# Latent attention on one core: two heads' keys in one tile, and score products in the halves of the array

## The chip, the cores and the metric

The kernel runs on one core of one Trainium2 chip. The metric is the device time of one execution in microseconds (us); less is better. Five engines run their own instruction lists and meet at semaphores: TensorE (PE, with its weight loads PEld), VectorE (DVE), ScalarE (ACT), GpSimd (POOL) and SyncE (SP).

## The reference

Two transformer layers on x of 1024 tokens by 256 features. The change touches the third of four blocks, the latent attention:

```python
    x = x + _layernorm(_L0_attn_ref(_layernorm(x, axis=-1), L0_attn_w_qkv, L0_attn_w_out), axis=-1)
    x = x + _layernorm(_L0_ffn_ref(_layernorm(x, axis=-1), L0_ffn_W_up, L0_ffn_W_gate, L0_ffn_W_down), axis=-1)
    x = x + _layernorm(_L1_attn_ref(_layernorm(x, axis=-1), L1_attn_Wdq, L1_attn_Wuq, L1_attn_Wdkv, L1_attn_Wuk, L1_attn_Wuv, L1_attn_Wo), axis=-1)
    x = x + _layernorm(_L1_ffn_ref(_layernorm(x, axis=-1), L1_ffn_lut, L1_ffn_gate_idx, L1_ffn_up_idx, L1_ffn_down_idx), axis=-1)
...
            c_kv = x @ Wdkv.T
            q = (x @ Wdq.T @ Wuq.T).reshape(B, T, nh, hs).transpose(0, 2, 1, 3)
            q_lat = jnp.einsum('bhtd,hdl->bhtl', q, k_eff)
            scores = jnp.einsum('bhtl,bsl->bhts', q_lat, c_kv) / jnp.sqrt(jnp.float32(hs))
            scores = jnp.where(causal[None, None, :, :], scores, jnp.finfo(scores.dtype).min)
            attn = jax.nn.softmax(scores, axis=-1)
            ctx = jnp.einsum('bhts,bsl->bhtl', attn, c_kv)
            y = jnp.einsum('bhtl,hld->bhtd', ctx, v_eff)
```

There are 16 heads of 16 features each, T is 1024, and the mask is causal.

## The kernel before

The whole program is written out by hand. Four lists of steps (`HEADS`, `FFN0`, `LATENT`, `FFN1`) are made before anything is issued; each engine walks the same lists in the same order and issues its part of each step. `order_of_latent` merges lists by hand-given costs, so the order of the work is fixed when the program is built. Matmul results go to PSUM banks that are handed out from a ring of six in the order of the list (`take_ring`); a bank comes free when the instruction that is marked for it has read it.

The latent attention works on eight pairs p of heads (2p and 2p+1). A head needs only 16 features, but each operand is kept as a high and a low part, so 48 or so of 64 partitions are in use for a head, and a pair fills 128 partitions: the even head the lower 64, the odd head the upper 64. For a pair:

- **project** (L1311): two matmuls of 512 columns for each half of the tokens, for q (`which` 0) and for k (`which` 1).
- q: ScalarE writes the rounded part to `R1` (L1603), VectorE writes the finished operand from the PSUM bank and `R1` with one instruction (L1920) to `QT(p)`. This frees the bank.
- k: ScalarE writes `R1` (L1603) and a second copy, `R2` (L1608, its tile is called `tern` in the trace). The bank is free after that. The keys are then `R2 - R1`, made by two instructions of 64 partitions each, one for each head: by VectorE for pair 0 (L1929), by GpSimd for pairs 1 to 7 (L2161). They go to two separate tiles, `KT[p % 4][:, 0]` and `[:, 1]`. Each tile has 128 partitions, of which the other head's 64 were set to zero (`keys_zero`, L2029). So a score product can take all 128 rows of q: the other head's q meets zeros.
- **row_max** (L1323): scores of 128 queries against up to 512 keys; VectorE adds the mask and takes the row maximum (L1947, with an instruction that reads the accumulator behind it). Even and odd head alternate in the list.
- **shift** (L1333, transposes): the maxima are turned, and VectorE subtracts them inside q (L1957).
- **weights** (L1344; L1369 for the last four heads): transposed scores, 128 keys against up to 1024 queries, in one or two products. ScalarE takes the exponential (L1617; L1627), GpSimd masks the diagonal block (L2168; L2175).
- **combine** (L1358; L1383): weights times values. Four heads stand side by side in the array's columns, 32 each (`tile_position=(0, 32 * j)`).

Three groups of four heads run this way, each beside the row maxima and projections of the pairs that come next; the last group runs beside the splitting of the weights of the next block (`split_gu`, `split_dn`). R1 has three buffers. `KT` has four pairs of tiles, so pairs 4 to 7 wait until the pair four before them is used up.

## Time and profile before

| | |
|---|---|
| median of 3 runs | 925.1 us (924.72 to 926.01) |
| profiled execution, span from first to last instruction | 923.3 us |
| TensorE busy | 832.7 us (90%), 4330 matmuls |
| VectorE busy | 766.5 us (83%) |
| ScalarE busy | 605.9 us (66%) |
| GpSimd busy | 430.6 us (47%) |

The profile is of one execution. Its own device time is not listed beside it; the three timed runs are 1.4 to 2.7 us above its span, which is what lies around the first and the last instruction. An engine is busy while it works on an instruction, also when that instruction is one of several in flight. The chain of work that ended last is followed back from the end: each piece was released by the piece before it, so its shares tell which engine set the time there. The latent attention runs from about 660 to 863 us of the span.

### The profile page before, as it was taken

To read this page: it belongs to the slowest core of one execution; us is meant where nothing else is said; L and a number is where in the kernel's file an instruction comes from. 1 tells how busy PE (TensorE), PEld (TensorE's weight loads), DVE (VectorE), ACT (ScalarE), POOL (GpSimd) and SP (SyncE) were. 2 spreads that over 40 slices of the span, in tenths; PEclk is the share of its full clock that TensorE was granted. 3 is DMA by queue.
4 is the path that set the end of the run, shared out by engine and by line. 5 is a ranking of instruction groups with operands and counts; after the bars stand their busy time and mean duration, and the time that the engine had idled before them with its cause. 6 is when DMAs were issued, how large, how long until landed. Compare 5 with 4: busy or idle time off the path is not lost.

```text
span 923.3 us, 13156 instructions
## 1 busy us (share of the span) xinstructions
PE 832.7 (90%) x4330; PEld 534.6 (58%) x4330; DVE 766.5 (83%) x1597; ACT 605.9 (66%) x1042; POOL 430.6 (47%) x455
## 2 busy tenths in 40 slices
PE   3889999999999999989899998679788999998997
PEld 2555665665665565655565565457555555554686
DVE  3788999889989999999899998585598687876637
ACT  5677767777777676766667767374545767657531
POOL 3134354354445277787667771171323434433301
PEclk9999999999999999999999999799989999999999
DMA  3388858966977667857857668130000000000001
GB/s 122 78 184 156 143 117 190 163 126 136 206 134 153 130 131 144 166 110 144 157 103 132 136 130 159 24 106 0 1 1 1 1 0 2 0 2 1 1 1 45
DMA packets 276867, 86.29 MB, mean 93 GB/s; under 512 B 267584, under 2 KB 272448, under 8 KB 276416
## 3 DMA queue, kind: packets, MB, share of 16 engines
q1 hardware_dynamic: 275520, 80.05, 44.8%
q0 software_dynamic: 992, 5.34, 1.9%
q8 instruction: 34, 0.56, 0.3%
q14 instruction: 33, 0.27, 0.1%
q10 hardware_dynamic: 288, 0.07, 0.0%
HBM read 17.29 MB, written 1.05 MB: 20 GB/s over the span
## 4 chain that ended last, share of the span: by engine, by line
PE 40%; DVE 37%; issue 9%; ACT 8%; DMA 3%; POOL 1%; SPq 1%; POOLq 0%; DVEq 0%; ACTq 0%
DVE EP L1762 9%; DVE nmax L1747 8%; PE ps L1097 7%; PE ps L1099 7%; PE ps L1098 7%; PE ps L1120 4%; DVE ptm L1861 3%; PE ps L1358 3%; PE ps L1344 3%; PE ps L1135 3%; PE ps L1323 3%; DVE ps L1947 2%; DMA ET<-EP 2%; DVE OL L1821 2%; DVE st L1661 1%
## 5 line engine op out<-in xcount | busy, mean ns | idle before, releaser
L1523 ACT ACTIVATE EP<-ps,rinv 128x1024 f16<-128x1024 f32 x128 | 142.2, 1112 | 44.5 <-DVE rinv L1757 42.9
L1762 DVE SCALAR_TENSOR_TENSOR EP<-ps,rinv,EP 128x1024 f16<-128x1024 f32 x128 | 163.3, 1276 | 2.4 <-ACT EP L1523 2.0
L1513 ACT ACTIVATE ps<-ps,nmax 128x1024 f32<-128x1024 f32 x128 | 139.2, 1088 | 35.7 <-DVE nmax L1747 35.2
L1747 DVE TENSOR_REDUCE nmax<-ps 128x1 f32<-128x1024 f32 x128 | 155.0, 1211 | 0.7 <-PE ps L1099 0.7
L1097 PE MATMUL ps<-KH,QH 128*128 128x512 f32 x256 | 115.4, 451 | 8.3 <-DVE KL L1729 4.2
L2106 POOL TENSOR_TENSOR wgu<-wgu,ptm 128x688 f32<-128x688 f32 x60 | 99.7, 1661 | 45.8 <-DVE ptm L1861 43.7
L1097 PE MATMUL ps<-ET,VH 128*128 128x512 f16 x256 | 98.7, 385 | 17.8 <-DMA ET<-EP 14.2
L1099 PE MATMUL ps<-KH,QL 128*128 128x512 f32 x256 | 100.8, 394 | 0.0
L2106 POOL TENSOR_TENSOR wdn<-wdn,ptm 128x512 f32<-128x512 f32 x45 | 57.7, 1282 | 92.2 <-DVE ptm L1861 91.0
L1098 PE MATMUL ps<-KL,QH 128*128 128x512 f32 x256 | 100.5, 392 | 0.0
L1098 PE MATMUL ps<-ET,VH 128*128 128x512 f16 x256 | 98.3, 384 | 0.0
L1099 PE MATMUL ps<-ET,VL 128*128 128x512 f16 x256 | 98.3, 384 | 0.0
L1617 ACT ACTIVATE ET<-ps 128x512 f32<-128x512 f32 (+3 forms) x144 | 62.6, 497 | 37.6 <-PE ps L1344 37.0
L1947 DVE CUSTOM_DVE_ANT_0 ps<-ps,tern 128x512 f32<-128x512 f32 (+3 forms) x128 | 71.9, 603 | 15.5 <-PE ps L1323 15.4
L2013 POOL TENSOR_TENSOR rs<-ve,mhalf 128x4 f32<-128x4 f32 (+2 forms) x22 | 19.8, 898 | 122.4 <-DVE ve L1666 98.2
L1097 PEld LDWEIGHTS ps<-KH,QH 128*128 128x128 f32 x256 | 48.2, 188 | 27.8 <-DVE EP L1762 8.1
L2168 POOL TENSOR_SCALAR_AFFINE_SELECT ET<-ET 128x128 f32<-128x128 f32 x96 | 28.1, 292 | 65.1 <-ACT ET L1617 58.3
L1097 PEld LDWEIGHTS ps<-ET,VH 128*128 128x128 f16 x256 | 25.8, 101 | 54.2 <-DMA ET<-EP 16.2
L1099 PEld LDWEIGHTS ps<-KH,QL 128*128 128x128 f32 x256 | 48.0, 188 | 11.1
L1097 PE MATMUL ps<-xh,wqh 128*128 128x512 f16 x128 | 49.8, 389 | 4.0 <-DVE KL L1729 3.4
L1098 PEld LDWEIGHTS ps<-KL,QH 128*128 128x128 f32 x256 | 48.3, 189 | 7.3
L1098 PE MATMUL ps<-xl,wqh 128*128 128x512 f16 x128 | 49.1, 384 | 0.0
(250 smaller groups left out, 2126.7 us busy)
## 6 DMA issues: line engine op xcount, KB each, us to landing
wqr<-in_wqk SPq DMA_DIRECT2D x16, 256.0 KB, 3.6
wgu<-in_tern POOLq DMA_DIRECT2D x3, 1024.0 KB, 6.1
wvr<-in_wv SPq DMA_DIRECT2D x8, 256.0 KB, 3.9
wor<-in_wo SPq DMA_DIRECT2D x16, 128.0 KB, 3.1
ET<-EP SPq DMA_TRANSPOSE x128, 4.3
X<-in_x SPq DMA_DIRECT2D x2, 512.0 KB, 5.7
prw<-in_down_idx POOLq DMA_DIRECT2D x2, 256.0 KB, 7.0
tern<-in_l_wuq_rep SPq DMA_DIRECT2D x1, 512.0 KB, 4.5
```

Source lines behind the costliest of these rows:

```text
L1097: e.matmul(dst, lh, rh, start=first, stop=False)
L1098: e.matmul(dst, lh, rl, start=False, stop=False)
L1099: return e.matmul(dst, ll, rh, start=False, stop=last)
L1120: mm = e.matmul(ps[:, 2 * r + o, :], l, m, start=i == 0, stop=i == len(pairs) - 1)
L1513: e.activation(bank, bank, ACT.Exp, bias=nmax[:, c:c + 1], scale=1.0, accum_out=rsum[:, c:c + 1]).then_inc(exped.sem, 1)
L1523: e.mul(EP[:, n % NE_RING, 0, :], SB(u, j), rinv[:, c:c + 1]).then_inc(e_hi.sem, 1)
L1617: e.activation(ET[:, r, c:c + n1], ps[:, BANK[(*step, c)][0], n - n1:n], ACT.Exp).then_inc(weight_exped.sem, 1)
L1747: e.tensor_reduce(nmax[:, c:c + 1], SB(u, j), AX.X, ALU.max, negate=True).then_inc(maxed.sem, 1)
L1762: e.scalar_tensor_tensor(out=EP[:, n % NE_RING, 1, :], in0=SB(u, j), scalar=rinv[:, c:c + 1], in1=EP[:, n % NE_RING, 0, :], op0=ALU.mult, ...
L1947: e.tensor_tensor_reduce(src, src, mask[:, m0:m0 + n], 1.0, -3.0e38 if part == 0 else half, ALU.add, ALU.max, NM[:, p % 2, i8, col:col + 1 ...
L2106: e.tensor_tensor(dst, dst, ptm[:, v % 2, 0:n], ALU.add).then_inc(lut_added.sem, 1)
L2168: e.affine_select(out=tile, in_=tile, compare_op=ALU.is_ge, fill=0.0, base=0, pattern=[[1, P]], channel_multiplier=-1).then_inc(masked.sem, 1)
```

## The change

The keys of a pair now lie in one tile of 128 partitions, even head below, odd head above, without zeros. So there are eight tiles, one for each pair, in the same memory. A score product takes only the 64 rows of its head and is placed in the lower or the upper half of the array's rows (`tile_position=(64 * hh, 0)`). The keys are split by one VectorE instruction straight from PSUM, as q is; `R2`, its ScalarE copies, the GpSimd subtractions and the zeroing are gone. The bank of a k projection is now freed by VectorE, not by ScalarE. The two weight tiles of the last block that lie in the same memory wait for other heads than before.

```diff
-             ("fold_k", 1), ("keys_zero", 3), ("split",), ("fold_v",), ("turn_in", b1, 1),
+             ("fold_k", 1), ("split",), ("fold_v",), ("turn_in", b1, 1),
...
-        KT = [QH, QL, KH, KL]
+        KT = [t[:, i, :] for t in (KL, QH, QL, KH) for i in range(2)]
...
-        GL = [KT[m // 2][:, m % 2, :] for m in range(4)]
+        GL = KT[0:4]
...
+        def rows_of(h):
+            return slice(64 * (h % 2), 64 * (h % 2) + 64)
...
-                if which == 0:
-                    r1_free[r] = q_split.mark(p, half)
-                    take_ring(step, q_split[p, half])
-                else:
-                    r2 = take(step, "r2", 2)
-                    R2_OF[step] = (r2, r2_free[r2])
-                    take_ring(step, k_lo_in.mark(p, half))
-                    for hh in range(2):
-                        token = (k_split_v if p == 0 else k_split_g).mark(2 * p + hh, half)
-                    r1_free[r] = r2_free[r2] = token
+                r1_free[r] = (q_split, k_split)[which].mark(p, half)
+                take_ring(step, r1_free[r])
...
-                    w.wait_ge(*k_split(h, 0))
-                    w.wait_ge(*k_split(h, (c + n - 1) // 512))
-                    e.matmul(ps[:, i, 0:n], QT(p)[:, i8 * P:i8 * P + P], KT[p % 4][:, hh, c:c + n],
-                             start=True, stop=True).then_inc(max_scored.sem, 1)
+                    w.wait_ge(*k_split[p, 0])
+                    w.wait_ge(*k_split[p, (c + n - 1) // 512])
+                    e.matmul(ps[:, i, 0:n], QT(p)[rows_of(h), i8 * P:i8 * P + P], KT[p][rows_of(h), c:c + n],
+                             start=True, stop=True, tile_position=(64 * hh, 0)).then_inc(max_scored.sem, 1)
...
-                        e.matmul(ps[:, i, 0:n], KT[p % 4][:, h % 2, k * P:k * P + P], Q2[p % 4][:, q0:q0 + n],
-                                 start=True, stop=True).then_inc(weighed.sem, 1)
+                        e.matmul(ps[:, i, 0:n], KT[p][rows_of(h), k * P:k * P + P], Q2[p % 4][rows_of(h), q0:q0 + n],
+                                 start=True, stop=True, tile_position=(64 * (h % 2), 0)).then_inc(weighed.sem, 1)
...
-                    if which == 1:
-                        r2, freed = R2_OF[step]
-                        w.each([freed])
-                        e.activation(R2[:, r2, :], bank, ACT.Identity, scale=pat[:, 5:6]).then_inc(k_lo_in.sem, 1)
...
-                    elif p == 0:
-                        r2 = R2_OF[step][0]
-                        w.wait_ge(*k_lo_in[p, half])
-                        w.wait_ge(*zeroed["keys", 0, 1])
-                        for hh in range(2):
-                            rows = slice(64 * hh, 64 * hh + 64)
-                            e.tensor_tensor(KT[0][rows, hh, cs], R2[rows, r2, :], f32(R1[rows, r, :]),
-                                            ALU.subtract).then_inc(k_split_v.sem, 1)
+                    else:
+                        w.wait_ge(*l1_hi[step])
+                        e.scalar_tensor_tensor(out=KT[p][:, cs], in0=ps[:, BANK[step][0], :], scalar=pat[:, 5:6],
+                                               in1=f32(R1[:, r, :]), op0=ALU.mult,
+                                               op1=ALU.subtract).then_inc(k_split.sem, 1)
...
-                    for h in range(8, 12):
+                    for h in range(4 * (m // 2), 4 * (m // 2) + 4):
                         w.wait_ge(*weighed[h, 7, "last"])
```

The GpSimd branch of L2148 to L2162 and `keys_zero` are removed as well, and the products of the last group (L1369) are changed as those of L1344.

**VectorE, the first projections of pairs 0 and 1** (the keys' tile is `QH` before and `KL` after, q's is `Q`; L1920 became L1898, L1947 became L1922). Before:

```order
L1682 TENSOR_TENSOR X<-X,XN 128x256 x2
L1929 TENSOR_TENSOR QH<-tern,R 64x512 x2
L1920 SCALAR_TENSOR_TENSOR Q<-ps,pat,R 128x512
L1661 BN_STATS st<-X 128x6 x2
L1664 BN_AGGR mv<-st 128x2 x2
L1666 TENSOR_SCALAR ve<-mv 128x2
L1672 TENSOR_SCALAR nm<-mv 128x2
L1920 SCALAR_TENSOR_TENSOR Q<-ps,pat,R 128x512
L1947 ISA ps,NM<-ps,tern 128x128
```

After:

```order
L1660 TENSOR_TENSOR X<-X,XN 128x256 x2
L1903 SCALAR_TENSOR_TENSOR KL<-ps,pat,R 128x512
L1898 SCALAR_TENSOR_TENSOR Q<-ps,pat,R 128x512
L1639 BN_STATS st<-X 128x6 x2
L1642 BN_AGGR mv<-st 128x2 x2
L1644 TENSOR_SCALAR ve<-mv 128x2
L1650 TENSOR_SCALAR nm<-mv 128x2
L1903 SCALAR_TENSOR_TENSOR KL<-ps,pat,R 128x512
L1898 SCALAR_TENSOR_TENSOR Q<-ps,pat,R 128x512
L1922 ISA ps,NM<-ps,tern 128x128
```

Two instructions of 64 partitions gave way to one of 128 for pair 0, and pair 1 has one ahead of its q that GpSimd did before.

**VectorE, the projections of pair 4 among the row maxima of pair 3** (738 to 744 us of the trace; the tile written for pair 4's keys is `QL` after). Before:

```order
L1920 SCALAR_TENSOR_TENSOR XH<-ps,pat,R 128x512
L1947 ISA ps,NM<-ps,tern,M 128x256
L1947 ISA NM 128x1
L1947 ISA ps,NM<-ps,tern,M 128x256
L1947 ISA NM 128x1
L1947 ISA ps,M<-ps,tern 128x512
L1947 ISA M 128x1
```

After:

```order
L1898 SCALAR_TENSOR_TENSOR XH<-ps,pat,R 128x512
L1922 ISA ps,NM<-ps,tern,M 128x256
L1922 ISA NM 128x1
L1922 ISA ps,NM<-ps,tern,M 128x256
L1922 ISA NM 128x1
L1903 SCALAR_TENSOR_TENSOR QL<-ps,pat,R 128x512
L1922 ISA ps,M<-ps,tern 128x512
L1922 ISA M 128x1
```

The split of the keys stands in line with the row maxima. The same happens twice for every pair from 2 to 7.

**GpSimd, from the first group on** (`ET` holds the exponentials that it masks). Before:

```order
L2161 TENSOR_TENSOR QL<-tern,R 64x512 x4
L2168 AFFINE_SELECT ET<-ET 128x128
L2161 TENSOR_TENSOR KH<-tern,R 64x512 x2
L2168 AFFINE_SELECT ET<-ET 128x128 x2
L2161 TENSOR_TENSOR KH<-tern,R 64x512 x2
L2168 AFFINE_SELECT ET<-ET 128x128 x6
```

After:

```order
L2113 AFFINE_SELECT ET<-ET 128x128 x96
L2120 AFFINE_SELECT ET<-ET 128x128
L2126 MEMSET KL 128x80
L2120 AFFINE_SELECT ET<-ET 128x128 x5
L2126 MEMSET KL 128x80
```

Only the masks are left, and the small memsets of `split_gu` stand behind the same masks as before. TensorE's list keeps its order and its number of matmuls; only operands and places in the array change.

## Rows read from the trace of the kernel before

**Rows 1.** Windows: length, then busy us of PE, PEld, DVE, ACT, POOL; clock; DMA.

```profile
660.00:711.00 51.00, 38.12 (x147) 24.91 (x146) 45.35 (x148) 27.66 (x50) 16.05 (x20) 0.93 0.00 1
711.00:830.00 119.00, 113.59 (x659) 65.83 (x657) 93.51 (x309) 79.33 (x171) 52.46 (x112) 0.99 0.01 1
830.00:863.00 33.00, 29.18 (x170) 13.64 (x170) 18.90 (x56) 25.01 (x60) 14.24 (x40) 1.00 0.00 1
```

**Rows 2.** Chain of work that ended last, by line: 711 to 830, 830 to 863 us.

```profile
by line: PE ps L1358 23.1%; PE ps L1344 21.5%; PE ps L1323 17.0%; DVE ps L1947 9.4%; issue 6.6%; ACT ET L1617 4.4%; ACT R L1603 3.9%; PE ps L1311 2.8%; PE ps L1333 2.7%; DVE XH L1920 1.9%; PE ps L1393 1.7%; DVE NM L1947 1.3%; ACT tern L1608
...
by line: PE ps L1383 29.2%; PE ps L1369 18.8%; issue 11.7%; DVE st L1661 8.3%; POOL rs L2013 6.4%; ACT XN L1411 4.4%; DVE Q L1957 3.9%; PE ps L1109 2.6%; DVE mv L1664 2.4%; PE ps L1393 1.8%; POOL ET L2175 1.8%; POOL nb L2018 1.5%; DVE XN L1
```

**Rows 3.** The same chain in 711 to 738, 763 to 781, 807 to 830 us.

```profile
by line: PE ps L1358 26.4%; PE ps L1344 26.2%; PE ps L1323 22.6%; PE ps L1311 5.2%; ACT ET L1617 4.2%; issue 4.1%; PE ps L1333 3.9%; DVE XH L1920 2.8%; ACT R L1603 2.6%; PE ps L1393 1.6%; ACT tern L1608 1.0%; ACTq L66 0.1%
...
by line: PE ps L1358 39.6%; PE ps L1344 29.3%; PE ps L1323 18.4%; PE ps L1333 6.1%; PE ps L1311 5.6%; PE ps L1393 2.4%; issue 0.0%
...
by line: PE ps L1358 34.4%; PE ps L1344 29.6%; PE ps L1323 22.2%; PE ps L1333 4.7%; POOL ET L2168 2.6%; PE ps L1311 2.0%; PE ps L1393 1.9%; issue 1.3%; ACT ET L1617 1.2%; ACTq L66 0.1%; POOLq L66 0.1%
```

**Rows 4.** Waits of VectorE, 711 to 830 us: us in total, times, longest.

```profile
DVE ps L1947 <- PE ps L1323: 22.7, 24, 2.3
```

**Rows 5.** Groups by form, 660 to 863 us: busy us, mean ns, idle before.

```profile
L1358 PE MATMUL ps<-ET,VX 128*32 128x512 f32 x144 | 18.3, 596 | 0.0
...
L1608 ACT ACTIVATE tern<-ps,pat 128x512 f32<-128x512 f32 x16 | 11.0, 685 | 0.0
...
L2161 POOL TENSOR_TENSOR KL<-tern,R 64x512 fp32r<-64x512 f32 x8 | 10.2, 1277 | 5.7 <-ACT tern L1608 5.4
...
L1344 PEld LDWEIGHTS ps<-Q,KL 128*128 128x128 f32 x24 | 4.4, 188 | 2.5 <-DVE M L1947 1.3 <-DVE XN L1970 0.4 <-ACT ET L1617 0.3
...
L1358 PEld LDWEIGHTS ps<-ET,VX 128*32 128x32 f32 x288 | 7.8, 108 | 10.8 <-issue 7.4 <-POOL ET L2168 2.2
...
L1929 DVE TENSOR_TENSOR QH<-tern,R 64x512 fp32r<-64x512 f32 x4 | 2.7, 686 | 1.9 <-ACT tern L1608 1.8
```

**Rows 6.** TensorE in order of time: start us, us, instruction.

```profile
819.56 0.45 PE L1344 MATMUL ps<-XL,QH 128*128 128x384 f32 x1
819.85 0.34 PE L1323 MATMUL ps<-KL,XH 128*128 128x384 f32 x1
820.02 0.33 PE L1344 MATMUL ps<-XL,QH 128*128 128x384 f32 x1
820.20 0.40 PE L1323 MATMUL ps<-KL,XH 128*128 128x256 f32 x2
...
828.89 0.28 PE L1344 MATMUL ps<-XL,QL 128*128 128x256 f32 x1
829.10 1.33 PE L1358 MATMUL ps<-ET,VX 128*32 128x256 f32 x16
```

**Rows 7.** Weight loads in the same place.

```profile
819.56 0.19 PEld L1344 LDWEIGHTS ps<-XL,QH 128*128 128x128 f32 x1 [0.84 <-DVE NM L1947]
...
820.03 0.36 PEld L1323 LDWEIGHTS ps<-KL,XH 128*128 128x128 f32 x2
```

**Rows 8.** The chain, piece by piece, 666 to 669 us.

```profile
666.03 0.58 ACT tern L1608
...
666.63 0.68 DVE QH L1929
...
668.07 0.75 DVE Q L1920
```

**Rows 9.** VectorE in order of time, 682 to 686 us.

```profile
682.27 1.40 DVE L1929 TENSOR_TENSOR QH<-tern,R 64x512 fp32r<-64x512 f32 x2 [1.02 <-ACT tern L1608]
...
684.68 0.75 DVE L1920 SCALAR_TENSOR_TENSOR Q<-ps,pat,R 128x512 fp32r<-128x512 f32 x1 [0.23 <-ACT R L1603]
685.35 0.56 DVE L1947 CUSTOM_DVE_ANT_0 ps<-ps,tern 128x384 f32<-128x384 f32 x1
```

**Rows 10.** Windows, as in rows 1: 710 to 720 us.

```profile
710.00:720.00 10.00, 9.74 (x45) 6.59 (x46) 7.04 (x24) 7.67 (x16) 2.89 (x7) 0.83 0.01 2
```

More of the change, by code:

```diff
@@ L262, in order_of_ffn0 @@
     todo += [("norm_in", b2, t) for t in range(4)]
-    todo += [("hidden", 6, 1), ("turn_in", b2, 0), ("hidden", 7, 1), ("keys_zero", 0), ("keys_zero", 1),
-             ("split",), ("point", "ffn0"), ("reuse", "ffn0")]
+    todo += [("hidden", 6, 1), ("turn_in", b2, 0), ("hidden", 7, 1), ("split",), ("point", "ffn0"), ("reuse", "ffn0")]
     return hidden_steps(0, todo)
@@ L342, in order_of_latent @@
     todo += norms("norm_out", 2, 4, 2)
-    todo += [("point", "latent"), ("keys_zero", 2), ("stats", 2, 0, 6, 2), ("latent", 0, 0), ("stats", 2, 1, 4, 2)]
+    todo += [("point", "latent"), ("stats", 2, 0, 6, 2), ("latent", 0, 0), ("stats", 2, 1, 4, 2)]
     todo += norms("norm_out", 2, 6, 2)
@@ L571, in build @@
         HEADS, FFN0, LATENT, FFN1 = order_of_heads(), order_of_ffn0(), order_of_latent(), order_of_ffn1()
-        def k_split(h, half):
-            return (k_split_v if h < 2 else k_split_g)[h, half]
         def added(t):
@@ L595, in build @@
         free_pair, free_single = {}, {}
-        count = {"work": 0, "scores": 0, "ring": 0, "pair": 0, "single": 0, "r1": 0, "r2": 0}
+        count = {"work": 0, "scores": 0, "ring": 0, "pair": 0, "single": 0, "r1": 0}
         def take(step, kind, n):
@@ L868, in build @@
                     zeroed.mark("ones")
-            elif what == "keys_zero":
-                POINT[step] = ended["PE"]
-                zeroed.mark("keys", *at, 0)
-                zeroed.mark("keys", *at, 1)
             elif what == "point":
@@ L876, in build @@
         free_ring = [free_pair[i][0] for i in range(3) for _ in range(2)]
-        R1_OF, R2_OF, r1_free, r2_free = {}, {}, [None] * 3, [None] * 2
+        R1_OF, r1_free = {}, [None] * 3
         ET_OF, ET3_OF, et_free, et3_free, et3_n = {}, {}, [None] * 10, {}, 0
@@ L899, in build @@
                 turn_in_banks(take_ring, *at)
-            elif what == "keys_zero":
-                POINT[step] = ended["PE"]
-                zeroed.mark("keys", *at, 0)
-                zeroed.mark("keys", *at, 1)
             elif what == "point":
@@ L1368, in _ @@
                     w.each([freed])
-                    e.matmul(ps[:, i, 0:n], KT[p % 4][:, h % 2, k * P:k * P + P], Q2[p % 4][:, hi - n:hi],
-                             start=True, stop=True).then_inc(weighed.sem, 1)
+                    e.matmul(ps[:, i, 0:n], KT[p][rows_of(h), k * P:k * P + P], Q2[p % 4][rows_of(h), hi - n:hi],
+                             start=True, stop=True, tile_position=(64 * (h % 2), 0)).then_inc(weighed.sem, 1)
                 elif what == "combine3":
@@ L2018, in stats @@
                 e.tensor_tensor(nb[:, o, ts], nm[:, o, ts], rs[:, o, ts], ALU.mult).then_inc(ln_shift.sem, 1)
-            def keys_zero(step, i):
-                w.wait_ge(*POINT[step])
-                if i == 3:
-                    w.wait_ge(*fold_lo["fold_k", 1])
-                w.wait_ge(*POOL_DONE[step])
-                for hh in range(2):
-                    rows = slice(64 - 64 * hh, 128 - 64 * hh)
-                    if hh == 1:
-                        w.wait_ge(*zeroed["keys", i, 0])
-                    e.memset(f32(KT[i][rows, hh, :]), 0.0).then_inc(zeroed.sem, 1)
             e.memset(mhalf[:, :], -0.5).then_inc(half_set.sem, 1)
@@ L2122, in _ @@
                     e.memset(vx4[:, :, :, 0], 1.0).then_inc(zeroed.sem, 1)
-                elif what == "keys_zero":
-                    keys_zero(step, *at)
                 elif what == "split_q":
@@ L2143, in _ @@
                     stats(*at)
-                elif what == "keys_zero":
-                    keys_zero(step, *at)
                 elif what == "reuse":
                     w.each(POINT[at[0]].values())
-                elif what == "project" and at[0] > 0 and at[1] == 1:
-                    p, _, half = at
-                    r, r2, cs = R1_OF[step][0], R2_OF[step][0], slice(half * 512, half * 512 + 512)
-                    w.wait_ge(*k_lo_in[p, half])
-                    w.wait_ge(*POOL_DONE[step])
-                    for hh in range(2):
-                        rows = slice(64 * hh, 64 * hh + 64)
-                        if hh == 1:
-                            w.wait_ge(*k_split_g[2 * p, half])
-                        if p > 3:
-                            w.wait_ge(*weighed[2 * p + hh - 8, 7, "last"])
-                        else:
-                            w.wait_ge(*zeroed["keys", p, 1])
-                        e.tensor_tensor(KT[p % 4][rows, hh, cs], R2[rows, r2, :], f32(R1[rows, r, :]),
-                                        ALU.subtract).then_inc(k_split_g.sem, 1)
                 elif what == "weights":
```

11 lines of the change are left out of this document (5 added, 6 removed).

## The prediction

> **What bounds the kernel now.** I read three views in this order: busy time by stretch, the chain that ended last, and the order of time inside a burst. By stretch [rows 1], the latent attention falls in three. From 660 to 711 us VectorE is busy 45.4 of 51 us and TensorE 38.1: VectorE sets the pace. From 711 to 830 us TensorE is busy 113.6 of 119 us, VectorE 93.5, ScalarE 79.3. From 830 to 863 us no engine is full. The chain says the same of the middle stretch [rows 2]: 21.5% and 17.0% of it are score products (L1344, L1323), 38.5% of 119 us or 45.8 us; the maxima on VectorE (L1947) have 9.4%. Of the last 33 us, 18.8% or 6.2 us are score products (L1369). The TensorE part is not spread evenly [rows 3]: in 711 to 738, 763 to 781 and 807 to 830 us the chain is nearly all TensorE, with products at 48.8%, 47.7% and 51.8%, which is 13.2, 8.6 and 11.9 us, together 33.7 us. VectorE waits 22.7 us for those products in the middle stretch [rows 4]. Between these phases lie bursts in which VectorE is on the chain.
>
> So the change takes work from TensorE where TensorE is short, and gives work to VectorE where VectorE has 25.5 us free in 119, but not evenly.
>
> **ScalarE and GpSimd.** 16 copies to `R2` of 685 ns go, 11.0 us [rows 5]; 28 subtractions of 1.28 us on GpSimd go too, with eight memsets. GpSimd is busy 52.5 of 119 us [rows 1] and appears on the chain with its masks only, so its removal is worth nothing in the sum. Its cover is that same idle time; without cover the masks behind a pair of subtractions would be 2.6 us late.
>
> **The keys on VectorE.** One instruction of this kind starts 0.67 us before the next thing (684.68 to 685.35, [rows 9]). 16 are added (10.7 us), four of 686 ns are removed (2.7 us) [rows 5]: +8.0 us of VectorE in all. Where it counts:
>
> - Pair 0, first half [rows 8]: today the chain goes through the `R2` copy (0.58), two subtractions (1.4) and then q's split at 668.07. After: `R1` is there at 666.03, keys 0.67, q's split near 666.7. That is 1.3 us earlier; pair 1's new split ahead of its own q gives back 0.7. Net -0.7.
> - Second half [rows 9]: VectorE waits 1.02 us for the `R2` copy, then 1.40 for the subtractions. After: no wait for the copy (-0.6), one split for pair 0 instead of two instructions (-0.7), one added for pair 1 (+0.7), and pair 1's q need not wait for ScalarE any more (-0.3). Net -0.9.
> - Pair 2, two splits in the stretch where VectorE is full: +1.3.
> - Pairs 4 and 6, two each, inside bursts of maxima in which VectorE runs without a gap: +2.7.
> - Pairs 3, 5 and 7 fall where VectorE waits for TensorE or ScalarE; six splits, 4.0 us, hidden under the 22.7 us of [rows 4]. If TensorE gets so fast that this cover is gone, all 4.0 count.
> - The `R2` copies of pairs 5 and 7 are on the chain as ScalarE pieces; about 0.6 us each for the first half: -1.2.
>
> The new wait is VectorE's for `R1` of the keys. Behind it stand maxima whose banks TensorE wants back. ScalarE writes `R1` well before VectorE arrives for pairs 2, 4 and 6, since VectorE is backlogged there, so I price it at nothing; the nearest row, q's wait of 0.23 us [rows 9], would give 14 x 0.23 = 3.2 us at the worst.
>
> **Score products in the halves of the array.** Nothing in this trace runs in row halves. The nearest thing is the column quarters of `combine`: 144 matmuls of 596 ns mean take 18.3 us in union, not 86 [rows 5], so four quarters do run at once. Today a product of 384 columns takes 0.18 us of the engine's time (820.02 to 820.20 [rows 6]), or 0.24 for 512. I went through TensorE's list with the rule that a product may start with its predecessor if it is of the other head, and otherwise after its own half is free. The list does not simply alternate (two products of one head, two of the other is common), so two halves do not mean half the time: in the middle stretch 277 products need 49.4 us now and 34.6 us then (0.70), in the last group 8.8 and 4.6 (0.52).
>
> Two prices are open. First, the weight load. A 32-column load lasts 108 ns and a 128-column one 188 [rows 5]: 80 ns for 96 columns, so 107 ns of the load path for a full one. If loads of the two halves can't overlap, no two products start less than 0.107 us apart, and the middle stretch needs 43.1 us (0.87), the last group 6.2. If they overlap, 34.6. The column quarters load and run together, so I take the second.
>
> The Trainium skill (TensorE: Matmul & The Clock Gate, Part 3) says that a weight load overlaps running matmuls when its row group differs, and that matmuls of different row groups start about 4 ns apart. No row here shows it for rows; by it a pair costs what one costs, and the sum would stay as it is.
>
> Second, the switch between arrangements. Before and after `combine` the engine changes from full width to quarters [rows 6, 7]. Into it: 0.21 us from product to `combine` (828.89 to 829.10) where 256 columns need 0.12, +0.09. Out of it: the first weight load starts together with its product at 819.56 instead of ahead of it (820.03 for 820.20), and the next product follows after 0.29 instead of 0.18 us, +0.11. If half rows are such an arrangement, each visit of a full-width step (project, shift, heads_out) among products pays both on both sides: 2 x 0.20 = 0.4 us. There are 31 visits in the middle stretch, 18 of them in the three TensorE phases, and 4 in the last group. The low bound is nothing per visit. I take 0.4, the row it is nearest to.
>
> The Trainium skill (TensorEngine Tiling (Array Packing), Key Properties) says that changing the tiling mode, not just the tile, drains the engine. It speaks against this change; no row shows it for rows. By it the visits are paid; without it the sum would be 10.1 us lower, before what VectorE takes back.
>
> **The sum.**
>
> - 660 to 711 us: -0.7 - 0.9 + 1.3 = -0.3. The visits there lie under VectorE's backlog.
> - TensorE phases: 33.7 x 0.30 = -10.1; 18 visits +7.2. Net -2.9.
> - Rest of the middle: 12.1 us of products on the chain x 0.30 = -3.6; 13 visits, a quarter of them on the chain, +1.3; VectorE +2.7; ScalarE -1.2. Net -0.8.
> - Last group: 6.2 x 0.48 = -3.0; 4 visits +1.6. Net -1.4. `split_gu` gains nothing: its memset on GpSimd stands behind the same mask.
>
> Together -5.4 us. The profiled span is 923.3 us and would become 917.9; with the 1.8 us around it that the median has, 925.1 becomes **919.7 us**.
>
> **The rivals.**
>
> *Free switching.* If a visit costs nothing, 7.2 + 1.3 + 1.6 = 10.1 us more are won. But then the middle stretch would last 119 - 3.7 - 8.5 = 106.8 us with VectorE at 93.5 + 6.7 = 100.2, 94% busy, which its waits today (22.7 us) do not suggest it can reach. I give it about half: 914. For: a row half uses the same columns as full width. Against: the +0.09 and +0.11 of [rows 6].
>
> *Loads one after another, with paid switches: slower.* Place: the score products of 711 to 830 us. Products are gained at 0.13 instead of 0.30: TensorE phases -4.3, rest -1.5, last group -1.8, which is 9.1 us less gained. 925.1 - 5.4 + 9.1 = 928.8. It decides from a price of 0.25 us per visit on: below that the 6.4 us that remain net are still a gain. For: 107 ns per full load is close to the 0.12 us of a 256-column product. Against: the quarters' loads do not queue.
>
> *No overlap at all.* The change then does not do what it says: 925.1 - 5.4 + 10.1 + 3.6 + 3.0 = 936.4.
>
> *The clock.* In 710 to 720 us the granted clock is 0.83 on average [rows 10]: part of it was at 1.2 instead of 2.4 GHz, after 700 to 710 us in which TensorE waited on VectorE's maxima. If products end sooner and TensorE stands still more in such places, more stretches like this follow. One costs up to 0.17 x 10 = 1.7 us where TensorE is on the chain; three more give 919.7 + 5.1 = 924.8.
>
> **How the numbers follow.** Chances: the forecast (916 to 923) 0.36; free switching 0.22; serial loads 0.22; clock 0.12; no overlap 0.05; the rest, waits for `R1` above all (up to 922.9), 0.03. The range of 911 to 930 reaches over free switching below and serial loads above and leaves out no overlap and the far tails; the likeliest case alone has 916 to 923. A measurement of this kernel can tell about 0.2%, 1.9 us, from no change. Faster (under 923.2): 0.34 + 0.21 + 0.03 = 0.58. Slower (over 927.0): 0.18 of serial loads, 0.05 of no overlap, 0.05 of clock, 0.01: 0.29. Within: 0.13.
>
> **What would show it.** Right: score products of the two heads whose starts lie a few ns apart; TensorE's union of L1323 and L1344 down by a third; VectorE's new splits 0.67 us apart from their neighbours; the stretch from the first weights to the last group shorter by 3 to 4 us. The visits: the first product behind a `project` has its weight load at its own start, not ahead. Wrong: starts never under 0.1 us apart (serial loads); no gap behind a visit (free switching, then nearer 914); VectorE's wait for L1323 gone and its busy share above 90% (then VectorE has become the bound and further TensorE gain is lost); the clock below 1.00 in more than the slices around 675 and 712 us.

## The result, and the profile after

The changed kernel takes 946.19 us (median of 4 runs, 944.85 to 946.74), the kernel before 925.56 us beside it (924.72 to 928.47). The ratio is 1.022, with a 95% interval of 1.020 to 1.024: slower by 2.2%, where 919.7 us was forecast and the range ended at 930. The profiled execution has a span of 944.1 us, 20.8 more than before. Of all the runs in this document one is left out of medians and ratios, because it was in a slower state of the chip: one of the four of e4 below, at 957.1 us.

The page of the changed kernel, its header, TensorE's busy time and the granted clock in 40 slices of 23.6 us:

```profile
span 944.1 us, 13073 instructions
...
PE 857.0 (91%) x4330; PEld 532.3 (56%) x4330; DVE 775.4 (82%) x1609; ACT 598.4 (63%) x1026; POOL 387.9 (41%) x419
...
PEclk9999999999999999999999997999796859689999
```

Of the eight slices from 661 to 850 us, in which the score products stand, six lie below full speed now, down to 0.5. Windows as in [rows 1], over the three stretches that answer to those rows (VectorE's, TensorE's, the last group):

```profile
664.00:714.00 50.00, 42.10 (x138) 23.94 (x137) 44.44 (x144) 23.09 (x41) 4.04 (x10) 0.77 0.00 1
...
716.00:851.00 135.00, 128.88 (x657) 62.89 (x655) 100.77 (x320) 74.12 (x161) 27.44 (x92) 0.76 0.00 1
851.00:884.00 33.00, 28.57 (x171) 11.03 (x171) 18.45 (x54) 25.17 (x60) 14.23 (x40) 1.00 0.01 1
```

The clock was 0.93 and 0.99 in the first two [rows 1] and is 0.77 and 0.76. The middle has grown from 119 to 135 us with the same instructions on TensorE. The last group is what it was. A clock of 0.76 means that 0.48 of a window ran at 1.2 GHz and the rest at 2.4. Added up over the record of the clock, from the first projection (664.3) to the first product of the last group (851.4), it is 88.7 us at 1.2 GHz, against 10.2 before (661.4 to 830.4). I call this the stretch below: 168.9 us before, 187.1 after. The whole difference is +2.9 us ahead of the stretch, +18.2 in it, -0.3 in the last group, and nothing behind (60.3 us in both).

Narrower windows of the changed kernel show the level, and what TensorE did ahead of it:

```profile
690.00:705.00 15.00, 12.96 (x49) 6.28 (x48) 12.91 (x42) 7.14 (x13) 0.59 (x2) 1.00 0.00 0
705.00:725.40 20.40, 19.84 (x60) 10.93 (x63) 16.80 (x56) 10.52 (x20) 2.35 (x8) 0.50 0.01 2
726.00:749.00 23.00, 21.42 (x138) 9.93 (x130) 17.69 (x55) 13.67 (x30) 5.29 (x18) 1.00 0.00 1
749.60:780.00 30.40, 29.81 (x105) 15.96 (x108) 21.20 (x67) 14.52 (x29) 4.12 (x14) 0.50 0.00 1
```

In 20.4 and 30.4 us TensorE runs at 1.2 GHz throughout, and is busy 97 and 98% of the time there: it is not standing still. In the stretch ahead of the first (690 to 705) it was busy 86%, and ahead of the second (726 to 749) 93%. The same work stands at 687 to 701 and at 719 to 741 us in the kernel before. Around the first TensorE is busy 81% there and in the second 95%, at full speed. Behind the first comes a fall of 3.4 us [rows 10], where the changed kernel has over 20; behind the second comes none, where the changed kernel has over 30 (the same work is in the third row):

```profile
686.00:710.00 24.00, 19.37 (x77) 11.56 (x76) 22.01 (x75) 11.53 (x22) 7.22 (x9) 1.00 0.00 1
719.00:741.00 22.00, 20.87 (x134) 12.37 (x129) 16.10 (x53) 14.64 (x32) 10.94 (x24) 1.00 0.00 1
741.00:765.00 24.00, 22.17 (x112) 12.39 (x110) 20.04 (x68) 15.74 (x32) 10.97 (x20) 1.00 0.00 1
```

The overlap itself came. TensorE in order of time in the changed kernel, score products of two heads (L1326 for the weights, L1305 for the maxima), at 1.2 GHz and then at 2.4:

```profile
719.52 1.22 PE L1293 MATMUL ps<-CS,QW 128*128 128x512 f32 x2
720.67 0.79 PE L1326 MATMUL ps<-XL,KL 64*128 64x512 f32 x1
720.67 0.79 PE L1305 MATMUL ps<-QH,XH 64*128 64x512 f32 x1
721.26 0.52 PE L1326 MATMUL ps<-XL,KL 64*128 64x384 f32 x1
721.71 0.79 PE L1293 MATMUL ps<-CS,KW 128*128 128x512 f32 x1
...
726.54 0.44 PE L1326 MATMUL ps<-XL,KL 64*128 64x384 f32 x1
726.55 0.38 PE L1305 MATMUL ps<-QH,XH 64*128 64x256 f32 x1
```

And the weight loads that belong to the first of these:

```profile
720.67 0.28 PEld L1326 LDWEIGHTS ps<-XL,KL 64*128 64x128 f32 x1 [0.65 <-DVE M L1922]
720.67 0.28 PEld L1305 LDWEIGHTS ps<-QH,XH 64*128 64x128 f32 x1
```

Two products start together, 7 ns apart in the single records (720.667 and 720.674), and so do their loads. That is what the Trainium skill says of different row groups (TensorE: Matmul & The Clock Gate, Part 3, with starts about 4 ns apart), and the trace agrees but for 3 ns. But the same product takes 0.79 us at 1.2 GHz, and the first load behind the full-width `project` (L1293) starts with its product, not ahead of it.

### The profile page after: what moved, and what is told of

The parts are those of the page before. It is cut to its first block, busy times and chain, and to the rows that moved or that the text cites. A ratio compares the mean times of both kernels' runs of the same rounds, so it can differ in the third digit from the quotient of the medians.

```text
span 944.1 us, 13073 instructions
## 1 busy us (share of the span) xinstructions
PE 857.0 (91%) x4330; PEld 532.3 (56%) x4330; DVE 775.4 (82%) x1609; ACT 598.4 (63%) x1026; POOL 387.9 (41%) x419
## 4 chain that ended last, share of the span: by engine, by line
PE 41%; DVE 36%; issue 9%; ACT 7%; DMA 5%; POOL 1%; SPq 1%; POOLq 0%; DVEq 0%; ACTq 0%
DVE EP L1740 9%; DVE nmax L1725 8%; PE ps L1079 7%; PE ps L1080 6%; PE ps L1081 6%; DMA ET<-EP 4%; PE ps L1102 4%; DVE ptm L1839 3%; PE ps L1326 3%; PE ps L1340 3%; PE ps L1305 3%; PE ps L1117 3%; PE ps L1293 2%; DVE ps L1922 2%; DVE OL L1799 2%
## 5 line engine op out<-in xcount | busy, mean ns | idle before, releaser
L1922 DVE CUSTOM_DVE_ANT_0 ps<-ps,tern 128x512 f32<-128x512 f32 (+3 forms) x128 | 71.6, 601 | 13.4 <-PE ps L1305 13.3
L1079 PEld LDWEIGHTS ps<-ET,VH 128*128 128x128 f16 x256 | 25.8, 101 | 54.8 <-DMA ET<-EP 17.2
```

Of the source, the lines that this page charges most:

```text
L1079: e.matmul(dst, lh, rh, start=first, stop=False)
L1922: e.tensor_tensor_reduce(src, src, mask[:, m0:m0 + n], 1.0, -3.0e38 if part == 0 else half, ALU.add, ALU.max, NM[:, p % 2, i8, col:col + 1 ...
```

## The experiments

In all of them the program ahead of the first projection and behind the last group is the same. "At 1.2 GHz" is the time at that level within the stretch of the profiled execution, and a switch is a change between a 64-row product and one of more rows in TensorE's list. Both the stretch and the time at 1.2 GHz come from one execution each, and they vary: by the mean clocks of the runs, a whole execution of the kernel before has 13 to 37 us at 1.2 GHz (its profile 25), the changed kernel 106 to 109, and e4 28 to 53 (its profile 53).

| run | median, us | ratio (95%) | stretch | at 1.2 GHz | 64-row switches |
|---|---|---|---|---|---|
| before | 925.6 | 1 | 168.9 | 10.2 | 0 |
| changed | 946.2 | 1.022 (1.020-1.024) | 187.1 | 88.7 | 131 |
| e1 halves only | 939.9 | 1.015 (1.012-1.018) | 183.0 | 61.4 | 131 |
| e2 full rows | 926.1 | 1.000 (0.998-1.002) | 169.7 | 10.2 | 0 |
| e3 one half | 956.8 | 1.035 (1.031-1.039) | 201.0 | 99.0 | 131 |
| e4 maxima in halves | 948.5 | 1.023 (1.019-1.027) | 193.8 | 41.0 | 208 |
| e5 weights in halves | 953.9 | 1.031 (1.028-1.034) | 194.6 | 34.1 | 183 |
| e6 rows 0 to 95 | 926.5 | 1.002 (1.001-1.004) | 170.7 | 17.1 | 0 |
| e7 pair 0 direct | 924.2 | 1.000 (0.998-1.001) | 167.5 | 3.4 | 0 |
| e8 rows 0 to 64 | 939.5 | 1.015 (1.011-1.020) | 182.0 | 54.6 | 0 |
| e9 even maxima | 941.5 | 1.019 (1.014-1.023) | 183.6 | 13.7 | 192 |
| e10 one tile, rows 0 to 64 | 942.9 | 1.018 (1.016-1.021) | 186.7 | 85.3 | 0 |
| e11 changed, again | 942.5 | 1.020 (1.015-1.024) | 190.1 | 102.4 | 131 |
| e12 halves only, again | 937.1 | 1.015 (1.010-1.020) | 182.5 | 58.0 | 131 |

**e1: the halves alone; e2: the keys alone; e3: one half.** e1 is the kernel before (tiles with zeros, GpSimd's subtractions, the copy to `R2`) with the score products in halves; e2 is the changed kernel with the score products at full width; e3 is the changed kernel with all of them in the lower half. The edits at the maxima (the weights' likewise):

```diff
 # e1, against the kernel before
-e.matmul(ps[:, i, 0:n], QT(p)[:, i8 * P:i8 * P + P], KT[p % 4][:, hh, c:c + n],
-         start=True, stop=True).then_inc(max_scored.sem, 1)
+e.matmul(ps[:, i, 0:n], QT(p)[rows_of(h), i8 * P:i8 * P + P], KT[p % 4][rows_of(h), hh, c:c + n],
+         start=True, stop=True, tile_position=(64 * hh, 0)).then_inc(max_scored.sem, 1)
 # e2, against the changed kernel
-e.matmul(ps[:, i, 0:n], QT(p)[rows_of(h), i8 * P:i8 * P + P], KT[p][rows_of(h), c:c + n],
-         start=True, stop=True, tile_position=(64 * hh, 0)).then_inc(max_scored.sem, 1)
+e.matmul(ps[:, i, 0:n], QT(p)[:, i8 * P:i8 * P + P], KT[p][:, c:c + n],
+         start=True, stop=True).then_inc(max_scored.sem, 1)
 # e3, against the changed kernel (and tile_position=(0, 0) at each product)
-    return slice(64 * (h % 2), 64 * (h % 2) + 64)
+    return slice(0, 64)
```

> The kernel before, with one edit: every score product takes only its head's 64 rows and is placed in that half of the array. The keys stay in their zero-padded tiles and are split by GpSimd as before. Theory A (the granted clock falls because of the products in row halves): TensorE at 1.2 GHz for tens of us between 660 and 863 us, and 15 to 22 us slower than before. Theory B (the keys on VectorE, and its waits, cost the time): within 3 us of before, or some us faster, mean clock as before (0.987).

> The changed kernel, but every score product takes all 128 rows at full width again. The pairs' tiles have no zeros, so a product sums the scores of both heads of the pair: this part of the computation is changed. Keys are split by VectorE from PSUM as in the changed kernel. Theory A: clock as before, no extra time at 1.2 GHz, time within -3 to +6 us of before (VectorE's 8 us more, mostly under its waits). Theory B: as slow as the changed kernel, +18 to +22 us.

> The changed kernel, but all score products, of even and odd heads alike, read rows 0 to 63 and are placed in the lower half of the array, so that none can run beside another. The odd heads then use the even head's operands: this part of the computation is changed. Theory A1 (what counts is that a product fills only half the rows): the clock falls at least as much as in the changed kernel, 20 us slower than before or more. Theory A2 (what counts is that overlapping products end sooner and leave TensorE standing still): products follow one another as before the change, the clock stays up and the time is within 8 us of before.

The loss is in the halves: e1 has 13.8 us of it by the medians (939.9 against 926.1 for the kernel before beside it), a little less than the 15 to 22 of theory A; e2 has none. Windows of e2 and e3, each over its stretch or a part of it:

```profile
659.00:828.00 169.00, 151.29 (x798) 88.57 (x797) 145.08 (x467) 95.98 (x201) 30.91 (x102) 0.97 0.00 1
```

```profile
752.00:785.00 33.00, 32.92 (x109) 18.68 (x107) 21.36 (x65) 14.68 (x29) 4.09 (x14) 0.50 0.00 1
```

With the keys on VectorE and full rows, VectorE has 145.1 us of work in 169 and the clock is 0.97, as before. With all products in one half, 33 us on end run at 1.2 GHz with TensorE busy 32.9 of 33. So it is not the overlap that pulls the clock down: without any overlap the time at 1.2 GHz is longer still.

**e4 and e5: one kind of product each.** The edit of e1 at the maxima alone (e4), and at the weights alone (e5).

> The kernel before, in which only the products for the row maxima read the 64 rows of their own head; the products for the weights read all 128 rows with zeros in the other half, as before. Theory A (every product in a row half lowers the TensorE work that holds the clock up): about half of what both kinds together did, which took the time at 1.2 GHz between the first projection and the last group from 10.2 to 61.4 us. So 25 to 45 us at 1.2 GHz and 929 to 937 us. Rival B (only the places count where row halves are already mixed with the narrow products of weights and values, so the weights' products do it alone): 10 us at 1.2 GHz and 924 to 927 us here, all of the loss in the run with the weights alone. Rival C (what costs is the switching between row halves and full rows, and the clock is a by-product): about 12 us of switches in all, half of them here, 930 us, with the 1.2 GHz time near 10 us.

> The other half of the same pair: the kernel before, in which only the products for the weights (of all pairs and of the last group) read the 64 rows of their own head; the maxima read all 128. Theory A: 25 to 45 us at 1.2 GHz, 929 to 937 us, and the losses of this run and of the one with the maxima alone add up to about that of both (14 us) or to less, if the clock falls only once both are thin. Rival B: all of it here, 61 us at 1.2 GHz and 940 us. Rival C: 930 us with the 1.2 GHz time near 10 us.

On the clock the profiles speak for theory A: 30.8 and 23.9 us more at 1.2 GHz, together 54.7, where both kinds at once (e1) gave 51.2. That the sum fits so well is partly luck, since another run of e4 had 25 us less at 1.2 GHz than its profiled one. On the time all three theories failed: 948.5 and 953.9 us, each of them slower than both kinds together. What had grown is the number of switches between 64-row and 128-row products, 208 and 183 instead of 131, because maxima and weights stand mixed in TensorE's list.

So I set TensorE's instructions of each run beside those of the kernel before, one by one (800 intervals from start to start), and added up the differences by what the interval leads from and to:

| us against before | neither in 64 rows | into 64 rows | within 64 rows | out of 64 rows | sum |
|---|---|---|---|---|---|
| changed | +12.9 | +6.4 | -8.7 | +7.4 | +18.0 |
| e1 | +11.5 | +7.1 | -10.5 | +5.9 | +14.0 |
| e3 | +12.8 | +7.5 | +6.8 | +5.0 | +32.1 |
| e4 | +9.2 | +9.7 | -9.0 | +14.9 | +24.8 |
| e5 | +8.2 | +9.8 | -0.3 | +8.1 | +25.8 |
| e9 | -0.3 | +5.4 | none | +9.5 | +14.7 |
| e10 | +17.8 | none | none | none | +17.8 |

The sums differ from those of the stretch by up to 0.2 us, by rounding. Time lost to the clock is in all the columns, and a little of the switches is in the first. Behind a 64-row product the two products of a `project` start 0.34 us apart at full clock in the changed kernel and 0.59 at 1.2 GHz; in e10, without switches, most stand at 0.23 and 0.43.

**e6 and e8: rows without halves.** All score products read rows 0 to 95, or 0 to 64, of 128 (the weights' likewise):

```diff
-QT(p)[:, i8 * P:i8 * P + P], KT[p % 4][:, hh, c:c + n],
+QT(p)[0:96, i8 * P:i8 * P + P], KT[p % 4][0:96, hh, c:c + n],   # e8: 0:65
```

> The kernel before, in which every score product (maxima and weights) reads rows 0 to 95 of both operands instead of 0 to 127, with no placement in the array's halves; rows 96 to 127 are left out of the sums, so the second head of a pair loses half of its operand. No two products can run beside each other. Theory A in its form that the clock goes by how many rows a product fills: a fall between full rows (10.2 us at 1.2 GHz, 926 us) and lower halves alone (99 us, 957 us); half way would be 50 us and 940 us. Rival D (it is the 64-row arrangement of the array that lowers the clock, whatever the number of rows): if 96 rows run in the full arrangement, about 10 us at 1.2 GHz and 924 to 928 us.

> The kernel before, in which every score product reads rows 0 to 64 of both operands, one row more than a half; rows 65 to 127 are left out of the sums, so the second head of a pair loses all but one row of its operand. If the clock goes by the number of rows that a product fills, 65 rows are as thin as the 64 of the run with lower halves alone: about 90 us at 1.2 GHz and, without switches between halves and full rows, 940 to 946 us. If it is the arrangement of the array in halves that lowers the clock, 65 rows run as 96 did (17 us at 1.2 GHz, 926.5 us): 10 to 20 us and 924 to 928 us.

The page's clock rows of e6 and of e8:

```profile
PEclk9999999999999999999999999899899999999999
```

```profile
PEclk9999999999999999999999998999895979899999
```

96 rows cost next to nothing (17.1 us at 1.2 GHz), which is what rival D had forecast. 65 rows, one more than a half and so not in halves, without a single switch, cost 13 us: 54.6 us at 1.2 GHz. That is less than the 90 that the theory of the rows asked for, but far from the 10 to 20 of rival D. So the rows count, and the arrangement is not needed for the fall. The fall lies between the run with 65 rows and the one with 96; where, was not tried.

**e7: pair 0's keys straight from PSUM, in the kernel before.**

```diff
-e.tensor_tensor(KT[0][rows, hh, cs], R2[rows, r2, :], f32(R1[rows, r, :]), ALU.subtract)
+e.scalar_tensor_tensor(out=KT[0][rows, hh, cs], in0=ps[rows, BANK[step][0], :], scalar=pat[rows, 5:6],
+                       in1=f32(R1[rows, r, :]), op0=ALU.mult, op1=ALU.subtract)
```

> The kernel before, in which the keys of pair 0 alone are split by VectorE straight from PSUM, with two instructions on 64 partitions each, and ScalarE's second copy of them is left out; everything else, tiles with zeros and full rows, is as before. If the copy lies on the way to the first products, as the chain of the kernel before reads, the first maxima start 1 to 2 us earlier and the time is 923.5 to 925 us. Rival: the first products wait for the queries as well, or the later norms take it back, and the time is within 0.2% of before (924 to 928 us). The time at 1.2 GHz stays near 10 us.

924.2 us, ratio 1.000 (0.998 to 1.001): no change that can be told. The first product of the maxima comes 7.0 us after the first projection, against 7.5 before.

**e9: switches with few thin rows.** Only the even heads' maxima read 64 rows.

```diff
+top = (64, 128)[hh]
-QT(p)[:, i8 * P:i8 * P + P], KT[p % 4][:, hh, c:c + n],
+QT(p)[0:top, i8 * P:i8 * P + P], KT[p % 4][0:top, hh, c:c + n],
```

> The kernel before, in which only the maxima of the even heads read the lower 64 rows (their own); all other products read 128 rows. Half as many products in halves as in the run with all the maxima, none of which can run beside another, but about as many switches between halves and full rows (some 208 between the first projection and the last group). If a switch costs 0.09 us, as product by product in the runs so far, that is 19 us, and the clock takes 5 us for 15 us more at 1.2 GHz: 944 to 952 us. Rival (the switches are free, and the losses so far are the clock's and of rows that wait): 928 to 932 us.

941.5 us (939.1 to 945.3): 14.6 above the kernel before beside it (926.96), and 3.5 us more at 1.2 GHz in the profile. This is the price of switches almost by itself, and it lies below my expectation's range and above the rival's. One place in e9, and behind it the same place in the kernel before, in order of time:

```profile
740.35 0.42 PE L1345 MATMUL ps<-XL,QL 128*128 128x384 f32 x1
740.70 0.50 PE L1324 MATMUL ps<-KL,XH 64*128 64x512 f32 x1
741.13 0.44 PE L1345 MATMUL ps<-XL,QL 128*128 128x384 f32 x1
```

```profile
734.66 0.42 PE L1344 MATMUL ps<-XL,QL 128*128 128x384 f32 x1
734.92 0.40 PE L1323 MATMUL ps<-KL,XH 128*128 128x512 f32 x1
735.16 0.37 PE L1344 MATMUL ps<-XL,QL 128*128 128x384 f32 x1
```

Into the 64-row product 0.35 us pass instead of 0.26, out of it 0.43 instead of 0.24. Over all such places at full clock where nothing waits, the medians are +0.09 us in and +0.19 us out, 0.28 for the pair. 96 pairs would be 27 us by the medians and 23 by the means (0.09 and 0.15: next to `combine` leaving costs only 0.10). TensorE is busy 20.3 us longer in the stretch; its idle time shrinks from 18.1 to 12.5 us, and so about 15 us arrive. The Trainium skill (TensorEngine Tiling (Array Packing), Key Properties) says that a change of the tiling mode drains the engine; the trace agrees in that a change between 128 and 64 rows costs time here.

**e10: the changed kernel with rows 0 to 64.** The edit of e8 in e2.

> The changed kernel (both heads' keys in one tile, split by VectorE) with every score product reading rows 0 to 64, one row more than the lower half: no halves, no switches, no two products beside each other. What is summed is the first head's scores and one row of the second's, for both heads. It differs from the run with all products in the lower half (99.0 us at 1.2 GHz, stretch of 201.0 us) only by the one row, and so by the arrangement; from the kernel before with rows 0 to 64 (54.6 us, 182.0 us) only by the keys, of which the odd heads' were zeros there. If the switches cost 0.085 us each and the clock goes by rows alone, the time is that of the lower halves less 131 x 0.085 = 11 us: 944 to 947 us, with 85 to 100 us at 1.2 GHz. If the arrangement (its switches or halves) lowers the clock too, or the zeros did nothing in the kernel before with 65 rows, the 1.2 GHz time is 50 to 60 us as there and the time 938 to 941 us.

942.9 us, below the 944 to 947 of the first theory, but with its 85.3 us at 1.2 GHz. Against e2 it is the cleanest pair of all: the same kernel, with 128 rows in e2 and 65 in e10, has 10.2 us at 1.2 GHz in one and 85.3 in the other. No product here runs beside another and nothing switches: the clock takes +17.8 us against the kernel before (+17.0 against e2), for 75.1 us more at 1.2 GHz, or 0.24 us for each. This rate is not exact. e8 gives 0.29 (13.1 us for 44.4), and the spread of the runs of one kernel, over the changed kernel and the twelve experiments together, gives 0.31, an estimate from their times and mean clocks. A window of e10:

```profile
698.00:725.00 27.00, 26.27 (x79) 18.98 (x81) 21.55 (x68) 13.28 (x26) 2.92 (x10) 0.50 0.00 1
```

**e11 and e12: the changed kernel and e1 once more, side by side.**

> The changed kernel once more, on the same chip as the next one, since the two were so far run on different chips: the time in that run was 946.2 us with 88.7 us at 1.2 GHz between the first projection and the last group, that of the next one 939.9 us with 61.4 us. If the difference is the kernels', it is 945 to 947 us again and 4 to 8 us above the next one; if it is the chip's, the two are within 2 us of each other.

> The kernel before with all score products in halves and nothing else of the change, once more, on the same chip as the changed kernel: 938 to 942 us and 55 to 70 us at 1.2 GHz if the difference of 6 us to the changed kernel is the kernels', within 2 us of the changed kernel if it was the chip's.

942.5 (941.1 to 950.0) and 937.1 us (936.2 to 945.1): 5.4 us apart again, with 102.4 and 58.0 us at 1.2 GHz in their profiles (the one of e11 is its longest run, 950.0). For the clock the difference is the kernels', not the chip's: the mean clock of the whole execution is 0.935 to 0.949 in the four runs of e11 and 0.954 to 0.967 in those of e12. For the time this is likely but not shown: the intervals of the two ratios overlap, and the time of e11 is below the 945 to 947 that I had expected.

## Why the prediction was wrong

**The step that failed is the rival of the clock**, in its mechanism and its size. I had taken the 0.83 of [rows 10] for the effect of TensorE's waits, priced three more such places at 1.7 us each, and gave it 0.12; the sum itself carried nothing for it. The runs show another cause: products that read 64 or 65 rows instead of 128. From e2 to e10 only the rows change, and the time at 1.2 GHz goes from 10.2 to 85.3 us. In e10 and in the changed kernel the clock stays at 1.2 GHz while TensorE is busy 97%, and in the kernel before it was at 2.4 while TensorE was busy 81%. Nor does TensorE stand still more: its idle time in the stretch is 14.1 us against 18.1 before. In the kernel before, the zeros in the other head's 64 rows kept all 128 rows in use; they looked like waste. What I had priced at 5.1 us costs about 0.24 x 78.5 = 19 us, an estimate by e10's rate, and 24 by the rate of 0.31. The Trainium skill (TensorE: Matmul & The Clock Gate, Part 1) lets the clock go by how busy the engine has been. The trace disagrees as far as that means busy time alone: more than 30 us at 1.2 GHz follow on 23 us in which TensorE was busy 93% and go on while it is busy 98%, where the kernel before ran 24 us at full speed with TensorE busy 81%. In its latent attention no matmul read fewer than 128 rows, so nothing there could show the fall. Nor did I allow for that: the range should have asked what is different in kind, not only what each instruction takes. The prediction's own sign of being wrong, a clock below 1.00 in more slices than those around 675 and 712 us, is the one that came.

**The sum by its terms**, for the middle and the stretch ahead of it:

- *Overlap.* Forecast: -10.1 and -3.6 in the middle. Right in kind, a little high. Against e3, which has the same rows and no overlap, the stretch of the changed kernel is 13.9 us shorter, some 2.5 of it by the clock (10.3 us less at 1.2 GHz, at e10's rate): about -11. The sign for it, TensorE's union of maxima and weights down by a third, did not come in the stretch (94.6 to 91.9 us, with the slow clock in it), but came in the last group at full clock (12.5 to 8.7).
- *Switches.* Forecast: 0.4 us per visit, +8.5 in the middle. Right in kind, the unit too high and the number of paid visits too low. In the changed kernel the medians at full clock are +0.084 us in and +0.088 out; 131 switches make about +11, or +9 by the means, since those next to `combine` cost nothing. Some 2.5 us more sit between the products of a `project` behind them. (With the part at 1.2 GHz the table has 6.4 + 7.4 = 13.8.) The free switching that I gave 0.22 is out: e9 loses 1.9%, nearly all by switches. "Nothing in this trace runs in row halves" had overlooked four products of 64 rows (L1261) in the block before, which show the price. In the kernel before, at full clock:

```profile
614.11 0.39 PE L1120 MATMUL ps<-XL,QL 128*128 128x512 f32 x1
614.42 1.12 PE L1261 MATMUL ps<-tern,B 64*128 64x512 f32 x2
615.48 0.50 PE L1120 MATMUL ps<-XH,QH 128*128 128x512 f32 x1
615.81 0.39 PE L1120 MATMUL ps<-XL,QH 128*128 128x512 f32 x1
616.04 0.40 PE L1120 MATMUL ps<-XH,QH 128*128 128x512 f32 x1
```

Products of L1120 start 0.23 us apart; into the 64-row pair 0.31 pass (+0.08), and behind it the first interval is 0.33 (+0.10). That is 0.2 for a visit, half of what I took; a `project` between 64-row products pays 0.3 in the changed kernel.
- So overlap and switches nearly cancel, -11 and some +12 by the places at full clock, and what is left of the +18.2 us of the stretch is the clock's, 19 us by e10's rate. The rate decides what full clock would have brought: with 19 us the halves would have won about nothing, with 24 us about 6. No run shows it, since none has halves at full clock. The forecast of -5.4 us may have been near for that case.
- *Last group.* Forecast -3.0 +1.6. Measured -0.3 (32.7 to 32.4 us), at full clock. The score products (L1351) have 10.7% of the 33 us of the chain, 3.5 us, where they had 6.2 [rows 2], which is the -3.0 nearly; what took it up is other work on the chain: ScalarE's exponentials (L1605) with 3.8%, GpSimd's masks (L2120) with 3.3% instead of 1.8 (L2175), and `combine` (L1365) with 30.3% instead of 29.2. The chain by line, 851 to 884 us:

```profile
by line: PE ps L1365 30.3%; issue 11.9%; PE ps L1351 10.7%; DVE st L1639 8.3%; POOL rs L1988 6.4%; ACT XN L1393 4.9%; DVE Q L1932 3.9%; ACT ET L1605 3.8%; POOL ET L2120 3.3%; PE ps L1091 3.1%; DVE mv L1642 2.4%; PE ps L1375 1.8%; POOL nb L1
```

- *Keys on VectorE.* Forecast: near nothing in the sum, with bounds by the waits for `R1`. Right: e2 is at 1.000 (0.998 to 1.002). The waits for `R1` did come, 7.5 us of VectorE ahead of key splits (L1903) in the rows below. That is more than the 3.2 that I had called the worst; but they were covered, since e2, which takes the same path of the keys, loses nothing. A split and the next instruction start 0.67 us apart (668.95 and 669.62), as forecast. The 1.3 us at the start came too (the first product of the maxima 6.1 us after the first projection instead of 7.5) and were gone by the end of the stretch; e7, which does only this, gives nothing either. Waits of VectorE in the stretch of the changed kernel (us, times, longest), and two rows of its order of time:

```profile
DVE ps L1922 <- PE ps L1305: 20.9, 20, 2.7
...
DVE KH L1903 <- ACT R L1585: 2.7, 2, 1.5
DVE QL L1903 <- ACT R L1585: 2.1, 2, 1.4
DVE QH L1903 <- ACT R L1585: 2.0, 3, 0.9
...
DVE KL L1903 <- ACT R L1585: 0.7, 2, 0.4
```

```profile
668.95 0.75 DVE L1903 SCALAR_TENSOR_TENSOR KL<-ps,pat,R 128x512 fp32r<-128x512 f32 x1 [0.24 <-ACT R L1585]
669.62 0.74 DVE L1898 SCALAR_TENSOR_TENSOR Q<-ps,pat,R 128x512 fp32r<-128x512 f32 x1
```

VectorE's wait for the maxima's products is still there, 19.9 of these 20.9 us in the middle (716 to 851 us) against 22.7 [rows 4]: VectorE did not become the bound.
- *660 to 711 us.* Forecast: -0.3. The clock was 0.77 there, and the first product of the weights stands 34.5 us behind the first projection, against 34.6 before. That looks as if the halves cost nothing here, but in e2, with the same path of the keys, it is 33.2: clock and switches took back the 1.3 us that the keys had won. In this part VectorE sets the pace, and most of the slow clock is hidden, which is part of why 1 us at 1.2 GHz costs less than half a us.

The other rivals: serial weight loads and no overlap are both out (loads of two heads start together). The range was wrong because the clock had been bounded by a count of three places that no row gave.

**What stays open.** The changed kernel and e1 give TensorE the same products, with the same rows and values, yet 89 to 102 us at 1.2 GHz in one and 58 to 61 in the other, and medians that are 5 to 6 us apart. Likewise e10 and e8, 85.3 against 54.6; there the odd heads' keys were zeros in e8, which may play a part. What in the path of the keys moves the clock was not found. Ahead of the stretch both profiles of the changed kernel are late by 3 to 4 us, with 6.8 us at 1.2 GHz near 610 us:

```profile
609.00:617.00 8.00, 7.06 (x20) 5.49 (x20) 5.66 (x14) 4.46 (x9) 6.95 (x9) 0.57 0.14 55
```

e2, e3 and e10 have the same code there and are not late. So the new path of the keys does not do it, and the cause of these 3 us, which are part of the measured loss, stays open.

## What to carry to other kernels

Row halves let two products of 64 rows run at once, but ask first what they do to the clock: a zero-padded product of 128 rows can be the cheaper one. Here the kernels with it had TensorE at 2.4 GHz for all but 10 of 169 us. Count the switches between 64-row and 128-row work in TensorE's list, not the products alone: a visit costs 0.2 to 0.3 us at full clock, and one overlapped pair of 512 columns saves at most the 0.24 that one of its products takes. When a change brings a form of instruction that its stretch of the trace does not have, search the whole trace for it first: here four products elsewhere held the price of a switch. Then test the form alone (e1 changes three matmul instructions), since four products could not show what many of them do to the clock.

## What was not expected of the hardware

- The granted clock fell further the fewer rows the score products read, with the same list of work: 10.2 us at 1.2 GHz in the stretch with 128 rows, 17.1 with 96, 54.6 with 65; with both heads' keys in one tile 10.2 with 128, 85.3 with 65 and 99.0 in one half of 64.
- Rows that multiply zeros kept the clock up as well as rows with data: the kernel before, with zeros in 64 of 128 rows, and e2, without zeros, both have 10.2 us at 1.2 GHz in the stretch.
- A product at 1.2 GHz takes 0.43 us per 512 columns instead of 0.24, but the kernel loses only 0.24 to 0.31 us for each us at that level. In e10 a part of it is taken up by TensorE's idle time in the stretch, 11.9 us instead of 18.1.
- At full clock, entering 64-row work costs 0.08 to 0.09 us in all the runs with switches (medians). Leaving it costs 0.19 in e9 and e4, where only maxima read 64 rows, and 0.08 to 0.09 in the changed kernel, e1, e3 and e5. Why it differs was not found.
